# A gated cross-attention block on one core: both contexts quantised straight into the low bytes of f16 words, and the first context's column sums taken in 32-column strips

## The reference

```
def fake_quant(x, scale, zp):
    q = clip(round(x / s + z), 0, 255)
    return (q - z) * s
x = x + tanh(g_xattn) * matmul(fake_quant(layernorm(x)), fake_quant(ctx))      # per batch
x = x + tanh(g_ffn) * (layernorm(x) @ (U * S @ V.T).T)
```

## Time and profile before

| | |
|---|---|
| median of three runs | 601.6 us (601.25 to 601.85) |
| profiled execution, span from first to last instruction | 600.8 us |
| its own time outside the span | not recorded apart; the median lies 0.8 us above the span |
| PE busy | 583.0 us, 97% |
| DVE, ACT, POOL busy | 64%, 35%, 32% |
| DMA moved | 102.74 MB, mean 171 GB/s; 387 GB/s from 15 to 60 us |

### The profile page before, as it was taken

One profiled execution on the slowest core, in us unless ns is written; L12 is line 12 of the kernel. 1 busy time (PEld: TensorE's weight loads), 2 busy tenths in 40 slices (PEclk: granted clock), 3 DMA queues, 4 the chain that ended last, 5 costly groups with the idle time before them and its releaser, 6 DMA issues.

```text
span 600.8 us, 7536 instructions
## 1 busy us (share of the span) xinstructions
PE 583.0 (97%) x2800; PEld 266.3 (44%) x2800; DVE 384.5 (64%) x703; ACT 210.5 (35%) x256; POOL 193.5 (32%) x149
## 2 busy tenths in 40 slices
PE   1999999999999999999999999999999999999998
PEld 0444444444444444445444444444444444444444
DVE  6968999995288962855266975647375665735212
ACT  4799877822041432476422220303011030301000
POOL 2998850002223419735505800210404030030000
PEclk9999999999999999999999999999999999999999
DMA  8999995539828896979934432360917355171512
GB/s 275 387 387 386 308 262 127 109 122 196 242 54 230 192 217 189 274 264 327 235 123 140 102 73 54 75 189 12 211 42 157 106 97 166 32 161 35 123 53 105
DMA packets 145940, 102.74 MB, mean 171 GB/s; under 512 B 108784, under 2 KB 109040, under 8 KB 145904
## 3 DMA queue, kind: packets, MB, share of 16 engines
q1 hardware_dynamic: 136912, 84.96, 53.6%
q10 hardware_dynamic: 8992, 17.30, 8.8%
HBM read 58.99 MB, written 16.78 MB: 126 GB/s over the span
## 4 chain that ended last, share of the span: by engine, by line
PE 74%; DVE 12%; DMA 7%; issue 3%; ACT 1%; SPq 1%; POOL 1%; ACTq 0%; DVEq 0%
PE bank L556 27%; PE bank L587 14%; PE bank L654 8%; PE bank L653 8%; PE bank L658 8%; PE bank L592 7%; DMA v_hl<-in_ctx_dram 4%; DVE u_hl L1249 2%; DVE ring L1134 2%; DVE xn L1171 1%; DVE xs L1174 1%; DVE v_hl L1243 1%; DMA qT<-qn 1%; PE bank L519 1%; DMA ring<-in_x_dram 1%
## 5 line engine op out<-in xcount | busy, mean ns | idle before, releaser
L556 PE MATMUL bank<-q,qT 128*128 128x512 bf16 x896 | 202.1, 381 | 0.6 <-DVE ring L1134 0.3
L556 PEld LDWEIGHTS bank<-q,qT 128*128 128x128 bf16 x896 | 87.7, 98 | 107.9 <-issue 1.8
L260 POOL TENSOR_SCALAR ring<-ring,bvec 128x2048 f32<-128x2048 f32 x16 | 33.3, 2084 | 270.2 <-DVE bvec L1116 270.2
L587 PE MATMUL bank<-v_hl,xT 128*128 128x512 f16 x512 | 115.8, 379 | 0.0
L265 POOL TENSOR_TENSOR ring<-ring,corr 128x512 f32<-128x512 f32 x64 | 88.7, 1417 | 24.6 <-ACT corr L851 23.6
L1134 DVE SCALAR_TENSOR_TENSOR ring<-bank,const,ring 128x512 f32<-128x512 f32 x64 | 47.6, 743 | 57.9 <-PE bank L556 57.8
L1207 DVE SCALAR_TENSOR_TENSOR ring<-bank,cy,ring 128x512 f32<-128x512 f32 x63 | 46.6, 747 | 56.7 <-PE bank L658 56.6
L654 PE MATMUL bank<-u_hl,hbuf 128*128 128x512 f16 x208 | 78.9, 380 | 0.0
L653 PE MATMUL bank<-u_hl,hbuf 128*128 128x512 f16 x208 | 78.9, 379 | 0.0
L254 POOL TENSOR_SCALAR q<-u8r,const 128x1024 bf16<-128x1024 uint8 x52 | 64.2, 1243 | 39.2 <-ACT u8r L757 35.6
L587 PEld LDWEIGHTS bank<-v_hl,xT 128*128 128x128 f16 x512 | 49.9, 98 | 59.9 <-DMA xT<-xs 0.5
(11 more groups left out here) (136 smaller groups left out, 524.9 us busy)
## 6 DMA issues: line engine op xcount, KB each, us to landing
out_dram<-ring SPq DMA_DIRECT2D x63, 256.0 KB, 3.6
ring<-in_x_dram SPq DMA_DIRECT2D x62, 256.0 KB, 4.1
v_hl<-in_ctx_dram SPq DMA_DIRECT2D x26, 512.0 KB, 11.5
stage<-in_ctx_dram ACTq DMA_DIRECT2D x17, 512.0 KB, 5.5
u_hl<-in_L_ffn_V_dram SPq DMA_DIRECT2D x8, 512.0 KB, 11.4
corr<-in_ctx_dram ACTq DMA_DIRECT2D x8, 512.0 KB, 6.1
stage<-in_ctx_dram SPq DMA_DIRECT2D x6, 512.0 KB, 11.4
q<-in_ctx_dram ACTq DMA_DIRECT2D x4, 512.0 KB, 10.1
```

The lines of the kernel that those rows point to most:

```text
L556: mm = nc.tensor.matmul(unit_bank(t, n)[:, :], qT_of(t)[:, k, :], q2[:, n, k, :], start=(k == 0), stop=(k == KT - 1))
L587: nc.tensor.matmul(h_bank(u)[:, :], xT[:, g, half, k % 8, :], v_hl[:, k, 0, :], start=(g == 0 and a == 0 and half == 0), stop=False)
```

## The change

Both contexts are kept as f16 words whose high byte is zero and whose low byte is the quantised number, which makes the word q x 2^-24. The high bytes are zeroed once by fills, and a chunk is then quantised in one step into the low bytes (a byte pattern of step 2). The zero point of the context is no longer subtracted (C_C2 becomes 0), and the factor 2^24 is put back at the eviction (C_AP) and in the column sums (0.25 / UNIT). For the first context ACT converts 14 chunks and POOL 18, DVE none. The second context keeps its ring of bytes; POOL copies them into the low bytes, with one more fill for block 3, where chunks had been staged. The first context's column sums are taken in strips, with column_parts, column_low and colsum_total. For tiles 0 to 2 the eviction comes first (x1_evict) and pre adds corr afterwards. The lists of all engines are changed around these, and the second identity matrix in f16 goes. Core of the diff:

```
+        UNIT = 2.0 ** -24
-        q2 = sb("q2", [P, NQ, KT, W], bf16)
+        q2 = sb("q2", [P, NQ, KT, W], f16)
+        ON_ACT = (6, 7, 8, 10, 12, 14, 16, 18, 20, 22, 24, 26, 28, 30)
+        POOL_FILLS = (0, 1, 3)
+        q2_low = lambda c: q2_chunk(c).bitcast(u8).rearrange("p (w b) -> p w b", b=2)[:, :, 0]
# gpsimd
+            def fill(n):
+                nc.gpsimd.memset(flat2(q2[:, n, :, :]).bitcast(f32), 0.0).then_inc(q2_filled, 1)
+            def op1(c):
+                pool.wait_ge(SPOT[c][1], LANDED[c])
...
+                nc.gpsimd.tensor_scalar(q2_low(c), flat2(SPOT[c][0]), C_R2, P_Z2, ALU.mult, ALU.add).then_inc(q2_pool, 1)
             def op2(c):
...
+                if c == CB + CQ * (NQ - 1):
+                    pool.wait_ge(ctx_u8, u8_count(ROOM_CHUNK))
+                    fill(NQ - 1)
+                    pool.wait_ge(q2_filled, 4)
+                nc.gpsimd.tensor_copy(q2_low(c), u8r[:, c % NU8, :]).then_inc(q2_pool, 1)
             def pre(t, n):
-                pool.wait_ge(x1_row, t + 1)
+                if t < G:
+                    pool.wait_ge(x1_ready, unit(t, n) + 1)
+                else:
+                    pool.wait_ge(x1_row, t + 1)
...
+            fill(0)
+            fill(1)
             for c in range(CQ):
-                if not on_dve(c):
-                    op2(c)
+                if c not in ON_ACT:
+                    op1(c)
             for n in range(NQ - 1):
-                for i, c in enumerate(range(CQ * (n + 1), CQ * (n + 2), 2)):
-                    op2(c)
+                for i, c in enumerate(range(CQ * (n + 1) + 1, CQ * (n + 2), 2)):
+                    op1(c)
                     if n == 0 and i < G:
                         pre_row(i)
+                if n == 0:
+                    fill(3)
                 for t in range(G):
                     pre(t, n)
# sync
             for c in range(12, CB):
                 load_chunk(c)
+            q_transpose(G)
             for i in range(CQ):
                 load_v(VORD[i])
-            q_transpose(G)
             u_load(2)
             u_load(3)
+            x_transpose(0)
             u_load(0)
-            x_transpose(0)
# tensor
+                    g = k % CG * GW
+                    mm = nc.tensor.matmul(colsum_bank(b, n)[g:g + GW, :], ones[:, g:g + GW], q2[:, n, k, :],
+                                          start=(k < CG), stop=(k >= KT - CG), tile_position=(0, g))
...
             for n in range(1, NQ):
                 for i in range(CQ):
-                    colsum(0, n, CK * i, CK * i + CK)
+                    if i % 2 == 1:
+                        colsum(0, n, CK * i - CK, CK * i + CK)
                     for t in range(G if n < NQ - 1 else 1):
                         s1_part(t, n, CK * i, CK * i + CK)
+                    if i == 2:
+                        colsum_total(0, n - 1)
             s1_part(1, NQ - 1)
-            s1_part(2, NQ - 1, 0, 8)
+            colsum_total(0, NQ - 1)
+            s1_part(2, NQ - 1)
+            s1_part(G, 0)
+            s1_part(G, 1)
             norm_sums(0)
-            s1_part(2, NQ - 1, 8)
-            s1(G)
+            s1_part(G, 2)
+            s1_part(G, 3)
             mm3(0)
# scalar
-            for j in VORD[0:5]:
-                v_square(j)
+            v_square(VORD[0])
+            v_square(VORD[1])
+            column_parts(0, 3)
+            v_square(VORD[2])
+            v_square(VORD[3])
             column_correction(0, 3)
-            for j in VORD[5:8]:
+            for j in VORD[4:8]:
                 v_square(j)
             root2(0)
+            x_hi(0)
             weight_root(0)
-            x_hi(0)
# vector
+                step(ts(C_C2, P_Z2, 0.0, None, ALU.mult))
+            nc.vector.memset(flat2(q2[:, 2, :, :]).bitcast(f32), 0.0).then_inc(q2_filled_dve, 1)
             for n in range(NQ - 1):
-                for i, c in enumerate(range(CQ * (n + 1) + 1, CQ * (n + 2), 2)):
-                    op2(c)
-                    if n == 0 and i == 1:
-                        sums1(3)
-                        variance1(3)
-                    elif n == 0 and i == 3:
-                        quantise(3)
                 for t in range(G):
-                    x1_unit(t, n)
+                    x1_evict(t, n)
+                column_low(0, n)
+                if n == 0:
+                    sums1(3)
+                    variance1(3)
+                    quantise(3)
+                else:
+                    for t in range(G):
+                        x1_stats(t, n - 1)
...
-            x1_unit(0, NQ - 1)
+            x1_evict(0, NQ - 1)
+            column_low(0, NQ - 1)
+            for t in range(G):
+                x1_stats(t, NQ - 2)
+            x1_evict(1, NQ - 1)
+            x1_evict(2, NQ - 1)
+            x1_stats(0, NQ - 1)
             variance2(0)
-            norm_sum_up(0)
             scale2(0)
-            norm(0)
-            x1_unit(1, NQ - 1)
-            x1_unit(2, NQ - 1)
             x_lo_half(0, 0)
             x_lo_half(0, 1)
+            x1_stats(1, NQ - 1)
+            x1_stats(2, NQ - 1)
             x1_unit(3, 0)
+            norm_sum_up(0)
+            norm(0)
             v_low(0)
             variance2(1)
             v_low(1)
             scale2(1)
```

More of the change, by code:

```diff
@@ L110, in gated_block_program @@
         (C_R1, C_R2, C_C1, C_C2, C_NC1, C_NC2, _, C_F2, C_TG1, C_TG2, C_AF1, C_AF2, C_A, C_AFF,
-         C_SMAX, C_SMIN, C_TV, C_EPS, C_WARM) = [const[:, i:i + 1] for i in range(19)]
+         C_SMAX, C_SMIN, C_TV, C_EPS, C_WARM, C_AP) = [const[:, i:i + 1] for i in range(20)]
         C_R, C_C, C_NC, C_F, C_TG, C_AF = [const[:, i:i + 2] for i in range(0, 12, 2)]
@@ L188, in gated_block_program @@
         part_count = lambda t, h=1: 2 * t + h + 1 if t < G else 2 * G + t - G + 1
-        WHOLE = (27, 31)
-        POOL_WHOLE = (1, 2, 3, 4, 5)
-        on_dve = lambda c: c in WHOLE or CQ <= c < CB and c % 2 == 1
-        act_u8 = lambda c: c + 1 - sum(i <= c for i in WHOLE + POOL_WHOLE)
-        dve_count = lambda c: sum(on_dve(i) for i in range(c + 1))
-        pool_count = lambda c: c + 1 - dve_count(c)
+        ON_ACT = (6, 7, 8, 10, 12, 14, 16, 18, 20, 22, 24, 26, 28, 30)
+        act_count = lambda c: sum(i <= c for i in ON_ACT)
+        pool_count = lambda c: c + 1 - act_count(c)
+        u8_count = lambda c: c - CB + 1
+        POOL_FILLS = (0, 1, 3)
         unit_bank = lambda t, n: bank[4 * (n % 2) + t] if t < G else bank[(unit(t, n) - NQ * G) % 3]
@@ L291, in _ @@
                         op2(c)
-                if t == G:
-                    pool.wait_ge(t_written, 2 * G)
-                    nc.gpsimd.memset(ident_h, 0.0).then_inc(ident_free, 1)
-                    pool.wait_ge(ident_free, 1)
-                    nc.gpsimd.affine_select(out=ident_h, in_=ident_h, compare_op=ALU.not_equal, fill=1.0, base=0,
-                                            pattern=[[-1, P]], channel_multiplier=1).then_inc(ident_ready, 1)
                 if t not in (6, 7):
@@ L734, in _ @@
             s1_part(8, 0)
-            colsum_total(NQ - 1)
+            colsum_total(1, NQ - 1)
             for n in range(1, NQ):
@@ L1014, in _ @@
             op2(9)
-            column_parts(3)
+            column_parts(1, 3)
             column_correction(1, 3)
@@ L1392, in _ @@
             y_unit(6, 3)
-            column_low(0)
-            column_low(1)
-            column_low(2)
+            for n in range(NQ - 1):
+                column_low(1, n)
             quantise(9)
@@ L1402, in _ @@
             y_unit(7, 3)
-            column_low(3)
+            column_low(1, 3)
             variance1(10)
```

224 lines of the change are left out of this document (106 added, 118 removed).

## The result

| | median | runs | ratio to before, 95% interval |
|---|---|---|---|
| before, beside it | 601.73 us | 601.25 to 602.82 (4) | |
| changed | 612.82 us | 612.6 to 613.11 (4) | 1.0182 [1.0167, 1.0196] |

The change makes the kernel 11.1 us slower. The prediction said slower, 608.5 us, by the mechanism that the trace shows. It is 4.3 us too low: 612.82 lies above the forecast's own range (605.6 to 611.2) and inside the whole range (599.0 to 613.0) only because that one leaves room for the rivals B and C.

The account below looks back on a forecast made before the run. PE, busy 97% of the span, bounds the kernel, but readiness of its inputs decides: +1.25 us to scale2(0)'s end and +5.65 behind it make +6.9, giving 608.5 us; own range 605.6 to 611.2, whole range 599.0 to 613.0.

Parts of the forecast that it names:

- B: Blocks 2 and 3: strided conversion costs POOL near 2.1 us, scale2(0) 4 to 5 us later; 613 us, chance 0.10.
- C: PE gaps at 39 us and in mm3(0) bring back the lower clock: 2.9 us more, 611.4 us, chance 0.15.
- A: Path behind scale2(0) isn't the last; PE carries its lead through: 599.0 us, at the most 593.3; chance 0.20.
- D: Whole kernel: V lands early, gaps shrink and the change cancels out, within 0.2%; chance 0.05.
- S, the end of scale2(0): After block 3: scale2(0) ends at 78.4 us, 1.25 us later than before; bounds 76.5 and 79.7.
- The opening: Start: fills make quantisation of tiles 0 to 2 0 to 0.6 us late; block 1 still begins at 35.1 us.
- the stall of 3.0 us in front of colsum_total(0,0): Block 1: PE arrives at 39.3 us and idles 3.0 us for column_low(0,0), ready at 42.3 us.
- The strips: First context's column sums: 64 strips priced at 3.82 us, 0.22 us per group of four.
- V's landing: Loads before scale2(0): q_transpose(3) goes ahead of V, so the last V lands near 75.1 us, 2.4 later.
- Behind S: From scale2(0)'s end to mm3(1): late norm(0) lengthens the chain by 5.65 us; bounds 4.7 and 7.0.
- The trace and the median: Whole kernel: 0.8 us added, the median 601.6 being that much above the profiled span of 600.8.
- The 8.3 us of work saved turn up as idle time: PE between 39 and 108 us: net 8.3 us of work removed becomes idle time.

Follow-up runs that it names:

- the early norm: Changed kernel with norm_sum_up(0) and norm(0) put back directly behind scale2(0), with what they need: 607.22 us.
- full sums: Changed kernel with the first context's column sums by full products again, without parts, low part and total: 615.76 us.
- the second fill: Changed kernel with POOL's fill(1) moved behind its conversions of block 0: 611.77 us.
- combination 1: Changed kernel with fill(1) late, norm(0) early, V loaded before q_transpose(3), x1_evict(3,0) between the halves of x_lo(0): 606.13 us.
- Combination 2: As combination 1, plus pre_row(2) ahead of chunk 13's conversion and POOL's third fill moved to DVE: 604.85 us.

## Why the prediction was right, and where its size was off

Right in sign and place. norm(0) behind x_lo(0), v_high behind norm(0), root2(1) behind eight v_high, and mm3(1) behind that, is what the trace shows (v_high at 92.16, after the 86 that was named; v_low(4) to (7) last), and the early norm gives back 5.6 us. B didn't occur: the strided conversion takes 1.20 us on POOL. A and D didn't either. C did, but within the wait: the 16 matmuls at 105.11 us came at the lower level in part, yet PE still waited 0.53 us for v_low and 0.52 us for the squares of U behind them, so mm3(1) was not held by the clock. The changed kernel in windows (columns as above): PE ran nothing from 100 to 102 us, and in the next two rows its granted clock is 0.67 and 0.50, the lower level.

```profile
100.00:102.00 2.00, 0.00 (x0) 0.00 (x0) 1.09 (x6) 1.97 (x5) 0.00 (x0) 1.00 0.41 159
102.00:104.00 2.00, 0.92 (x2) 0.13 (x2) 2.00 (x2) 2.00 (x3) 0.00 (x0) 0.67 0.00 0
104.00:106.00 2.00, 1.84 (x6) 0.62 (x6) 1.97 (x3) 1.97 (x4) 0.00 (x0) 0.50 0.00 0
106.00:108.00 2.00, 2.00 (x11) 0.92 (x10) 2.00 (x3) 2.00 (x4) 0.00 (x0) 0.98 0.28 56
```

The Trainium skill, "TensorE: Matmul & The Clock Gate", section "Why this matters for your kernels", warns that idle gaps between bursts bring the lower clock back. The granted clock of these rows agrees; in the kernel before no gap was long enough to show it.

That 612.82 lies in the stated range is luck in part. Neither B nor C, for which the range was widened, set the time, and two errors of 3 us in the opening nearly cancel each other.

The 4.3 us between 608.5 and 612.8 come from these terms:

- **S, the end of scale2(0): +3.5 instead of +1.25.** Three errors stand behind it.
  - The opening. "The quantisation of tiles 0 to 2 is 0 to 0.6 us late" and block 1 from 35.1 us, bounds 1 us to either side: block 1 starts at 38.57, 3.5 us late. The fills took 3.47 us on DVE and 3.51 on POOL, as priced (3.2 to 4.5); what the prediction had no term for is that a fill on POOL stops DVE. In exchange the stall of 3.0 us in front of colsum_total(0,0) shrank to nothing.
  - The strips, at 0.22 us for a group of four. That price came from line 523 in the second context, where long rows of strips run back to back (the row behind this list, kernel before: 48 in 2.70 us). Between products a group costs 0.43 us: in the rows of block 1 above, four products start at 39.00 and the strips follow at 39.96 instead of 39.86, and the next product comes 0.33 us after them. Blocks 1 to 3 take 38.5 us, of which 0.3 is waiting; the prediction's own prices without waits give 35.5 (11.7, 11.7 and 12.1). Once the opening and the stall are set against each other, this difference of 2.7 us is the largest part of the excess. Over all 16 groups and eight totals PE's work falls by the 4.7 us of the page and not by 8.3.
  - V's landing, the other candidate for S, decided nothing. The squares were held by the total of block 3 on ACT's list and ended at 79.4, and the root behind them holds DVE for 0.33 us.

```profile
305.12 2.77 PE L523 MATMUL bank<-q,ones_b 128*32 128x512 bf16 x48
```

For the end of tile (2,3) in sum: +3.5 for the opening, -3.0 for the stall, +2.7 for the strips, -0.4 and -0.7 for two waits that came out smaller (colsum_total(0,2), chunk 17) make about +2; measured +1.9 (77.1 against 75.2), and 0.3 for the root. Block 1 ended at 51.1 (forecast 50.0), block 2 at 63.6 (61.7 to 63.1).
- **Behind S: +7.0 instead of +5.65**, the upper bound. The prediction has POOL busy with pre_row(3) and pre(3,n) until about 84; it is busy until 89.2. So both subtractions of x_lo(0) ran at 2.17 us beside it, where one of two was taken, and the first steps took 1.42 and 1.64 instead of 0.8. norm(0) ended at S + 11.5, not S + 9.95 (9.0 and the added 0.95); 0.2 of the difference came back in ACT's and DVE's lists behind it.
- **The trace and the median: +1.0.** The prediction took the 0.8 us between the span of 600.8 and the median of 601.6 for the time outside the span. That time is 1.8 us in both kernels, and the profiled execution of the kernel before was about 1.0 slower than its median. Where in that trace the 1.0 us lies isn't known.
- Behind mm3(1) 0.3 us came back.

3.6 + 1.0 - 0.3 = 4.3 us. Small slips in the recorded text change nothing: 37.5 + 1.2 + 2.0 is 40.7, and the DMA row is at 8 or 9 until 90 us, not 70. Rival C's stretch from 17.1 to 22.8 us has matmuls 0.43 us apart, but the granted clock of its rows reads 1.00, so that its level there is read from the spacing alone. "The 8.3 us of work saved turn up as idle time" held in kind and not in size: 4.7 us were saved, the strips are worth 2.9 us where they stand (full sums), and the orders that came with them cost more.

What stays open: about 5.6 us of the 11.1 are the norm's place and 1.1 the second fill, and these two add up (combination 1). Combination 2 brings back 8.0 in the median, and some 3 us stay. The trace points at the order of block 3: before, scale2(0) needed of block 3 only unit (0,3); now it stands behind the evictions of (1,3) and (2,3), and DVE waits 3.13 us for PE's tile (2,3) (the row at 77.36). No run puts x1_stats(0,3) and scale2(0) ahead of them, nor ACT's last squares, which end at 79.4, ahead of the correction of block 3 in this kernel.

## What to carry to other kernels

Work taken from the busiest engine is worth what the next wait leaves of it: look first at what sets the end of the stretch. Replacing 64 full matmuls by strips added four round trips over three engines, and each hop waits behind whatever stands ahead of it in a list; count those hops before the matmuls saved. Price a small matmul group from a row where it stands between the same neighbours: here 0.43 us between products against 0.23 in a long row. And when an instruction is moved back in one engine's list, follow the longest row of work that it releases on the next engine: here one small norm moved behind 10 us of DVE work moved 8.4 us of ACT work with it.
